# Cross-attention decoder layer: wide maximum behind the halves, keys turned ahead of the maxima, FFN rows turned behind an output unit

## The reference

```python
q_r = jnp.einsum('bshq,hqr->bhsr', q_big, W_qr)
k_r = jnp.einsum('bld,hdr->bhlr', kv_r, W_kr)
scores = jnp.einsum('bhsr,bhlr->bhsl', q_r, k_r)
attn = jax.nn.softmax(scores, axis=-1)
ctx_c = jnp.einsum('bhsl,bld->bhsd', attn, kv_r)
ctx_lat = jnp.einsum('bhsd,hkd->bhsk', ctx_c, w_kc_kv)
...
x1 = _bitlinear(x, w1)
x2 = _bitlinear(x, w2)
hidden = jax.nn.sigmoid(x1) * x2
return _bitlinear(hidden, w3)
```

## Time and profile before

| what | us |
|---|---|
| median of 3 runs | 2365.67 (2363.03 to 2366.86) |
| profiled execution | 2365.12 |
| its span, first to last instruction | 2363.3 |
| TensorE busy in matmuls | 2220.1 (94%), mean granted clock 0.964 |
| GpSimd busy | 1829.2 (77%) |
| VectorE busy | 1688.6 (71%) |
| ScalarE busy | 1197.9 (51%) |
| largest group on GpSimd, sums L1768 | 1138.7 in 315 |
| exponentials L1798 | 605.6 in 768 |
| context L2151 | 550.5 in 2816 |

### The profile page before, as it was taken

The page is one execution under the profiler, slowest core; times in us unless marked ns, Lnnn a source line. Parts: engine busy times, 40 slices in busy tenths (PEclk is TensorE's granted clock), DMA queues, the critical chain, the costliest instruction groups (busy, mean ns, idle before and its releaser), DMA issues. The chain is left out here.

```text
span 2363.3 us, 47265 instructions
## 1 busy us (share of the span) xinstructions
PE 2220.1 (94%) x15390; PEld 1416.5 (60%) x15390; DVE 1688.6 (71%) x2771; ACT 1197.9 (51%) x1933; POOL 1829.2 (77%) x818
## 2 busy tenths in 40 slices
PE   7989858999996999999999999999999999999798
PEld 4545446777772555555555555555555555555587
DVE  6888847888875667667667667667667767767775
ACT  4323222222222666666666666666666666665243
POOL 3554527988983799999999999999999999989211
PEclk9889978999996999999999999999999999999999
DMA  4000024666676344324334333333333432431011
GB/s 143 22 15 28 15 73 138 191 180 187 190 195 152 79 93 99 96 65 98 87 74 96 81 82 89 84 87 81 83 95 74 89 96 67 96 90 39 22 47 41
DMA packets 239505, 216.16 MB, mean 91 GB/s; under 512 B 124500, under 2 KB 213768, under 8 KB 239304
## 3 DMA queue, kind: packets, MB, share of 16 engines
q1 hardware_dynamic: 239432, 215.22, 35.8%
HBM read 129.68 MB, written 60.78 MB: 81 GB/s over the span
## 5 line engine op out<-in xcount | busy, mean ns | idle before, releaser
L1768 POOL TENSOR_TENSOR x_acc<-x_acc,x_prob 128x1600 f32<-128x1600 f32 x315 | 1138.7, 3615 | 26.0 <-ACT x_prob L1798 2.1
L1798 ACT ACTIVATE x_prob<-x_scores 128x800 f32<-128x800 f32 (+1 forms) x768 | 605.6, 838 | 70.5 <-PE x_scores L2118 60.7
L2151 PE MATMUL x_context<-x_prob,x_kv 128*64 128x400 f32 x2816 | 550.5, 512 | 7.0 <-ACT x_ctxs L1838 6.7
L1910 DVE TENSOR_REDUCE x_mx<-x_ring 115x2 f32<-115x1024 f32 x310 | 380.1, 1226 | 50.7 <-PE x_ring L2218 30.9
L1919 DVE TENSOR_REDUCE x_mx<-x_ring 115x1 f32<-115x466 f32 (+3 forms) x352 | 221.8, 630 | 240.3 <-PE x_ring L2225 240.0
L1818 ACT COPY x_half<-x_ring 115x466 f32<-115x466 f32 (+3 forms) x352 | 190.0, 540 | 312.9 <-PE x_ring L2225 312.8
L2151 PEld LDWEIGHTS x_context<-x_prob,x_kv 128*64 128x64 f32 x2816 | 171.3, 136 | 241.5 <-issue 232.5
L2118 PE MATMUL x_scores<-x_qh,x_dh 64*128 64x400 f32 (+1 forms) x1536 | 272.4, 349 | 0.3 <-ACT x_prob L1798 0.3
L2118 PE MATMUL x_scores<-x_ql,x_dh 64*128 64x400 f32 (+1 forms) x1536 | 267.1, 341 | 0.0
L2118 PE MATMUL x_scores<-x_qh,x_dl 64*128 64x400 f32 (+1 forms) x1536 | 267.0, 342 | 0.0
L1923 DVE TENSOR_REDUCE x_mx<-x_half 115x1 f32<-115x466 f32 (+3 forms) x352 | 220.2, 626 | 4.4 <-ACT x_half L1818 1.4
(11 more groups left out here) (206 smaller groups left out, 3637.0 us busy)
## 6 DMA issues: line engine op xcount, KB each, us to landing
scratch_qh<-q_qsh SPq DMA_DIRECT2D x64, 200.0 KB, 3.2
scratch_ql<-q_qsl SPq DMA_DIRECT2D x64, 200.0 KB, 3.5
x_qm<-scratch_qh SPq DMA_DIRECT2D x64, 200.0 KB, 3.6
x_qh<-scratch_qh SPq DMA_DIRECT2D x64, 200.0 KB, 3.3
x_ql<-scratch_ql SPq DMA_DIRECT2D x64, 200.0 KB, 3.7
x_rden<-scratch_rden SPq DMA_DIRECT2D x64, 200.0 KB, 3.5
scratch_kr<-q_krot SPq DMA_DIRECT2D x32, 384.0 KB, 2.3
x_kr<-scratch_kr SPq DMA_DIRECT2D x32, 384.0 KB, 4.6
```

Of the source, the lines that this page charges most:

```text
L1768: pool.tensor_tensor(acc[0:rows, parity], first, prob[0:rows, c % PR], ALU.add).then_inc(acc_done.sem, 1)
L1798: act.activation(prob[0:rows, c % PR, u * HALF:(u + 1) * HALF].rearrange("p (j s) -> p j s", j=2), psc[0:rows, u, :, 0:BANK], ACT.Exp).the ...
L1910: dve.tensor_reduce(best[0:block_rows(r), :, r, i], src[0:block_rows(r), :, 0:b - a], AX.X, ALU.max).then_inc(read_sem(u), 1)
L2151: mm = pe.matmul(pav[DC * s:DC * s + DC, j, 0:BANK], kv[0:rows, parity, c], prob[0:rows, c % PR, cols], start=c == 0, stop=c == LC - 2)
```

## The change

- In chunk 11 of a cross-attention slot the half pair now stands ahead of the scores and the wide maximum behind them, as in the other chunks. ScalarE's copies and VectorE's waits follow.
- In TensorE's list alone, "turn" 0 and "mT" change places behind the context of chunk 11. The list of the other engines and the banks stay: mT, turn 0, out, turn 1.
- x2 and its semaphores belong to Opening; the wait for the last two stores moves from the end of cross-attention to the load of the FFN's last group.
- The normalising of the FFN's second group moves from the end of cross-attention to the start of VectorE's first FFN slot.
- In the FFN, TensorE does the output unit of chunk 3 ahead of the turn of the next rows.

```diff
--- before.py
+++ after.py
@@ -1483,7 +1483,6 @@
         rden = sb("rden", [P, 2, BANK])
         ctxn = sb("ctxn", [P, 2, BANK])
         xr = sb("xr", [S, 2, E])
-        x2 = sb("x2", [S, 2, E])
 
         psc = ps("scores", [P, 2, 2, 512])
         pav = ps("context", [P, 2, 512])
@@ -1496,22 +1495,23 @@
         order = []
         for c in range(LC):
             own = []
-            r, i = next(narrow) if c > 0 else (None, None)
-            pair = [("half", r, i, 0), ("half", r, i, 1)] * (c > 0)
-            own += pair if c < LC - 1 else [next(wide)]
+            if c > 0:
+                r, i = next(narrow)
+                own += [("half", r, i, 0), ("half", r, i, 1)]
             own += [("scores", 0), ("scores", 1)]
             if c == 2:
                 own += [("den",), ("turn", 2)]
-            elif 0 < c < LC - 1:
+            elif c > 0:
                 own.append(next(wide))
-            elif c == LC - 1:
-                own += pair
             own.append(("context",))
             if c == LC - 1:
                 own += [("mT",), ("turn", 0), ("out",), ("turn", 1)]
             order.append(own)
         assert next(wide, None) is None and next(narrow, None) is None
         beside = [[u for u in own if u[0] not in ("scores", "context")] for own in order]
+        *_, at_end = order
+        i, j = at_end.index(("mT",)), at_end.index(("turn", 0))
+        at_end[i], at_end[j] = at_end[j], at_end[i]
         units = [u for own in beside for u in own]
         first_max, *_ = [u for u in units if u[0] in ("max", "half")]
         *_, last_max = [u for u in units if u[0] == "max"]
@@ -1555,7 +1555,7 @@
         xr_loaded = transfer("xr_loaded", 16, 16)
         m_stored = transfer("m_stored", 16)
         m_loaded = transfer("m_loaded", 32)
-        x2_stored = transfer("x2_stored", 16, 32)
+        x2, x2_stored = f.x2, f.x2_stored
 
         dh_copied = sig("step_high_copied", 3, 5)
         kh_copied = sig("keys_copied_down", 3, 5)
@@ -1724,8 +1724,6 @@
             slot(B - 1, 1)
             store_x2(B - 2, 0)
             store_x2(B - 1, 1)
-            for parity in range(2):
-                sp.wait_ge(x2_stored.sems[parity], x2_stored.done(B - 2 + parity, parity))
 
         @block.gpsimd
         def _(pool):
@@ -1840,8 +1838,7 @@
             def slot(n, parity):
 
                 for c in range(LC):
-                    if c < LC - 1:
-                        copy_halves(n, c)
+                    copy_halves(n, c)
                     if c == 1 and not is_at(n, -1) and not is_at(n, 0):
                         save_context(n)
                     if is_at(n, -1) and 3 <= c < 3 + H // 2:
@@ -1849,11 +1846,7 @@
                         act.copy(wco[:, c - 3], pav[:, c % 2, 0:E]).then_inc(wco_copied.sem, 1)
                     if not is_at(n, -1):
                         for u in range(2):
-                            if c == LC - 1 and u == 1:
-                                copy_halves(n, c)
                             exponentials(n, c, u)
-                    elif c == LC - 1:
-                        copy_halves(n, c)
                     for u in beside[c]:
                         if u[0] == "den":
                             save_den(n)
@@ -1946,8 +1939,6 @@
                             half_maximum(n, u)
                         elif u[0] == "mT":
                             wait_read(dve, n, last_max)
-                            wait_read(dve, n, (*copied[-1][:3], 0))
-                            dve.wait_ge(half_read.sem, half_read.at(n, len(copied)))
                             dve.tensor_reduce(negm[:], mx[:], AX.X, ALU.max, negate=True).then_inc(max_ready.sem, 1)
                             turn_maxima(n)
                     if c == 6 and not is_at(n, -1):
@@ -2016,13 +2007,6 @@
                     dve.bn_aggr(f.mv[:, b], f.stats[:, b]).then_inc(f.row_mv.sem, 1)
                 dve.wait_ge(f.row_mv.sem, f.row_mv.at(1, GB))
                 dve.tensor_scalar(f.veps[:], f.mv[:, :, 1], EPS, None, ALU.add).then_inc(f.row_veps.sem, 1)
-
-            def normalise_second():
-                dve.wait_ge(f.row_rstd.sem, f.row_rstd.at(1, 1))
-                dve.wait_ge(f.xn_turned.sem, f.xn_turned.at(0, EC))
-                for b in range(GB):
-                    dve.tensor_scalar(f.xn[:, b], f.x[:, 1, b], f.mv[:, b, 0:1], f.rstd[:, b:b + 1],
-                                      ALU.subtract, ALU.mult).then_inc(f.xn_ready.sem, 1)
 
             def split_rows():
                 for i in range(EC):
@@ -2082,7 +2066,6 @@
                 last_context(j)
             second_rows()
             output(B + 1, 1)
-            normalise_second()
 
         @block.tensor
         def _(pe):
@@ -2341,6 +2324,8 @@
         self.xh = sb("xh", [P, 2, EC, GT], F32R)
         self.xl = sb("xl", [P, 2, EC, GT], F32R)
 
+        self.x2 = sb("x2", [S, 2, E])
+        self.x2_stored = Transfer(ctx, nc, "x_x2_stored", 32)
         self.loaded = sig("weights_loaded", 0)
         self.constants = sig("constants_set", 0)
         self.quant = sig("quantising_steps", 0)
@@ -2407,6 +2392,9 @@
             def load(k, parity):
 
                 sp.wait_ge(x_kept.sem, x_kept.at(k - 2, 1))
+                if is_at(k, NG - 1):
+                    for last in range(2):
+                        sp.wait_ge(f.x2_stored.sems[last], f.x2_stored.done(B - 2 + last, last))
                 src = d["x2"][bass.ds(k * GB, GB)].rearrange("b s e -> s b e")
                 sp.dma_start(x[:, parity], src).then_inc(x_loaded.sems[parity], 16)
 
@@ -2530,6 +2518,8 @@
 
             def slot(k, parity, more):
                 for m in range(FC):
+                    if m == 0 and is_first(k):
+                        normalise(k + 1, 1 - parity)
                     gate(k, m)
                     if m >= 1:
                         low(k, parity, m - 1)
@@ -2586,10 +2576,10 @@
                 pe.wait_ge(x_low.sem, x_low.at(k, EC))
                 for m in range(FC):
                     hidden(k, parity, m)
+                    if 1 <= m <= GB and not is_first(k):
+                        output(k - 1, 1 - parity, m - 1)
                     if m == 3 and more:
                         turn_xn(k + 1)
-                    if 1 <= m <= GB and not is_first(k):
-                        output(k - 1, 1 - parity, m - 1)
 
             pe.wait_ge(f.quantised.sem, 2)
             for_groups(pe, slot)
```

## The result

| kernel | median us | runs | ratio to before (95% interval) | slot of the loop, us | FFN group, us |
|---|---|---|---|---|---|
| before | 2365.05 | 5 | | 44.80 | 16.55 |
| changed | 2352.34 (2351.53 to 2353.04) | 5 | 0.9948 (0.9934 to 0.9963) | 44.58 | 16.91 |

The account below looks back on a forecast made before the run. TensorE's stream was taken as the bound. From the profiled 2365.12 us, -9.0 -0.45 -1.4 -1.65 +2.0 = -10.5 gave 2354.6; with 0.55 us for the median of runs, 2355.2 us, range 2350.5 to 2361.

Parts of the forecast that it names:

- slots of images 0 to 29: Cross-attention slots that turn keys: each gains 0.30 us, 9.0 us in all, bounds 4.5 and 12.
- slot of image -1: First cross-attention slot, which has no scores: its gain was left at zero.
- The order of the maxima: End of a cross-attention slot, half pair first: TensorE's holes of 0.41 and 0.23 us go, context 0.10 us closer.
- the first rival: Cross-attention: VectorE's wide maximum ends 0.15 to 0.30 us late, costing 4.5 to 9 us, 2359.7 to 2364; 20%.
- The uncovered copy: Cross-attention slot end: output product waits for VectorE's copy of the maxima, 0.62 us behind their turn; 0.44 us come back.
- The exchange: Chunk 11 of cross-attention, keys turned before maxima on TensorE: takes back about 0.2 us of the new order's gain.
- The last slot with maxima: Last cross-attention slot with maxima, where no keys are turned: gains about 0.45 us.
- The start of the FFN: Step from cross-attention to FFN: store wait and normalising leave, GpSimd is late next, FFN starts 1.4 us earlier.
- The clock: Head of the FFN: after a shorter idle time TensorE's clock stays up, gaining 1.65 us, bounds 0 and 1.65.
- The FFN: Chunk 3 of six FFN groups: output unit waits for VectorE's bank read, 0.33 us lost each, 2.0 us in all.
- the rival of 1.8 us a group: FFN: the later turn is passed on in full, 10.9 instead of 2.0 us lost, 2364.1 us; 5%.
- The rival on TensorE's clock: Cross-attention loop: clock falls behind each slot's new 0.44 us hole, 1.65 us per fall, 2394 us; 5% with all unseen.

## Why the prediction was right

The time was forecast as 2355.2 us in a range of 2350.5 to 2361.0; 2352.34 was measured. Part of the agreement is luck. Without the 2.1 us of the unchanged phases the gain is 10.6 us, against 10.5 forecast, but errors of both signs met in it: the loop's slots and the clock gave some 3 us less than forecast, the slots of images -1, 0 and 1 some 3 us more.

| step | forecast, us | measured, us |
|---|---|---|
| slots of images 0 to 29 | 30 x 0.30 = 9.0 | 8.9: 27 x 0.217 = 5.9, images 0, 1 and 29 3.0 |
| slot of image -1 | 0 | 0.8 |
| slot of image 30, to its negation | 0.45 | 0.4 |
| start of the FFN | 1.4 | 1.5 |
| clock at its head | 1.65 | 0.9 |
| FFN groups | -2.0 | -2.2 |
| unchanged phases | 0 | 2.1 |

**The order of the maxima**: right to some hundredths. Forecast were wide maximum 1.40 us behind the pair, context 1.72, turn of the keys 3.23, maxima 3.72; measured 1.44, 1.77, 3.26, 3.75. VectorE's negation was ready when TensorE came. TensorE and VectorE did not meet within 0.01 us in front of the turned keys: VectorE's wide maximum ended at 1074.82, 0.15 us before TensorE came. So the condition of the first rival, a wide maximum later than worked out, did not arise; the slot fell short for the next reason.

**The uncovered copy**: the mechanism was right, its size is the term that was off. I took 0.62 us from the last slot with maxima; in the loop it is 0.70. That slot is unrolled, and there the wait for the copy stands on the product's weight load; in the loop it stands on the queue's instruction ahead of the load, and the product starts 0.13 instead of 0.05 us behind the copy, as the run with the exchanged waits shows. The row was of the right thing but of another form of it. 30 x 0.08 = 2.4 us is the difference.

**The exchange**: I said that it takes back about 0.2 us of what the new order gives. It takes back 0.36 us (2.68 against 2.32): the run without it has slots of 44.23 instead of 44.58 us. Two errors met there: the 0.62 us for the gap in the changed kernel, and a step from the maxima to the turn of 0.18 us, which is 0.10 us in the run where TensorE didn't wait for the maxima. And I took the exchange's price for one and the same in all slots: image 0's slot gains by it where the order of the maxima is the new one, as the run without it shows.

**The last slot with maxima**: wrong. It gained 0.4 us up to the negation, but only 0.2 us from one output product to the next, where 0.45 was forecast. There the output product waits for GpSimd in the changed kernel, which I had excluded from the loop's row and not looked up for this slot:

```profile
2145.22 0.26 PE L2213 MATMUL x_ring<-f_ident,x_negm 115*14 115x115 f32 x1
2146.41 0.86 PE L2191 MATMUL x_ring<-x_wco,x_ctxn 128*100 128x256 f32 x3 [0.93 <-POOL x_ctxn L1748]
...
2145.25 2.00 POOL L1748 TENSOR_TENSOR x_ctxn<-x_ctxs,x_rden 128x400 f32<-128x400 f32 x2
```

From the first unit of chunk 11 the maxima are turned 0.74 us earlier than in the kernel before (3.46 instead of 4.20), and the product starts 1.19 us behind them instead of 0.62. In the loop the normalised half is ready some 0.6 us before the product starts, here it is the last event. The first slots gained more than forecast: images -1 and 0 together gave 2.6 us to the negation of image 1, where the slot before image 0 was taken as zero. The run without the exchange shows that half of it goes with the exchange, in part or wholly by the earlier rise of the clock.

**The start of the FFN**: right, both late arrivals went and GpSimd was next. TensorE's rest shrank by 1.4 us, as forecast. The 1.5 us of the table are of the whole stretch behind the last negation, which took 62.9 us in the changed kernel and up to 63.8 us in runs with the same code there, so the last digit is chance.

**The clock**: it stayed up, but the forecast of 1.65 us counted TensorE alone. The change's own normalising, beside GpSimd's copy of the rows, took 2.90 instead of 1.38 us and held the first gate: its tanh ended at about 2210.0 and the gate started at 2210.5. I had named this collision and allowed it 0.1 to 0.2 us; it was 0.5, because the first of the four instructions alone took 1.93 us. With the normalising behind the gate the second group came another 0.3 us earlier (11.68 instead of 12.00). The 0.4 us that are then still missing are not traced.

**The FFN**: right in place and size, 0.36 for 0.33 us. The rest in front of the tanh of chunk 4 went from 1.73 to 0.94 us, and the later turn was not passed on, so the rival of 1.8 us a group did not come.

**The rival on TensorE's clock**, that short idle times in each slot make it swing: the loop's clock is 1.00 in the changed kernel, with an idle time of 0.44 us in each slot. (Its 2394 us for a fall in each slot is added up wrongly: 30 x 1.65 us on top of 2355.2 are 2404.7. And half of the first rival's 20% stands in the sum of chances as 0.08 instead of 0.10.) No run here shows the swing that the Trainium skill ("TensorE: Matmul & The Clock Gate", "A second HAM failure mode: psum-queue depth-cycling") tells of.

## What to carry to other kernels

Before a piece of work is moved into an idle time, ask what it covers where it stands: here 0.23 us were filled and 0.44 us opened, because the same turn had hidden the read that the next instruction needs. A filler is worth only as much as its own inputs allow; look up who reads the bank it writes, and where that read stands in the other engine's list. The same filler can gain in one place and lose in another: ahead of image 0's slot, where it stood in front of a wait of 1.9 us and not 0.2, 1.3 us were gained with it, though part of that may be the clock. And a row taken as the price of a wait must come from the same form of code: here the loop's wait cost 0.08 us more than the unrolled one, because the late wait stood on another instruction.

## What was not expected of the hardware

- It matters where the wait that comes late stands in front of a TensorE instruction: 0.05 us from the end of what is waited for if it is on the product's weight load, 0.13 to 0.15 us if it is on the queue's instruction ahead of that. Which of two waits lands where differs between the loop and the unrolled slots of the same program text.
- VectorE's scaling of 100 x 256 values, 0.40 us alone, took 1.93 us when it started 0.1 us behind a copy of 100 x 1024 on GpSimd (1.89 us); it ended 0.15 us behind the copy.
- TensorE's clock fell behind a rest of 1.93 us in one trace and not in seven others with rests of 1.78 to 1.95 us, and behind 3.3 us in both. The length of the rest alone doesn't decide: in the slot of image 1 it fell to 0.50 for 3.4 us behind idle times of 1.8 and 2.3 us in two traces, and not behind 2.8 us in a third.
- The end of the program behind the last group's first matmul takes 27.8 us in the three traces whose clock falls only in the last 4 us, 29.3 to 29.6 in the six that have 3.4 us more at the lower level, and 30.6 in the one with 6.8 us more. A difference of 1 to 3 us between two traces can be this alone.
- The traces differ by up to 3 us in one slot, that of image 1: 45.1 to 48.5 us between its negations, the two longest being those with the fallen clock. There VectorE waits for a load of denominators, and TensorE behind it (kernel before, TensorE, VectorE and SyncE's queue):

```profile
842.27 0.48 PE L2218 MATMUL x_ring<-x_kh,x_qm 64*115 64x512 f32 x2 [1.44 <-DVE x_mx L1919]
...
841.44 0.25 DVE L1892 RECIPROCAL x_few<-x_few 100x16 f32<-100x16 f32 x1 [2.30 <-DMA x_few<-scratch_den]
...
830.28 0.75 SPq L1660 DMA_DIRECT2D scratch_den<-x_dens  x1
839.97 0.29 SPq L1663 DMA_DIRECT2D x_few<-scratch_den  x1
```

The denominators are stored and then loaded back. In this slot the store stands on SyncE behind the weights w3, whose issue occupies that queue for 9.5 us, and is issued 5.2 us later in the slot than in the next one. The larger part comes behind it: the load back is issued 9.7 us behind the store, where the next slot takes 1.7 us (871.60 to 873.33). That w3's load is the cause of both follows from its place alone; no run moved it, and it stays open.
